# The state part of a fused sandwich block reordered, and its decay rows made by bf16 matmuls of the transposed sums

## The chip, the cores and the metric

One core of one Trainium2 chip runs the whole program. The metric is device time in microseconds (us) from the program's start to its end. Engines: PE (TensorE), DVE (VectorE), ACT (ScalarE), POOL (GpSimd), and SP, which issues the DMAs.

## The reference

The input is 8 sequences of 1024 tokens with 256 features. A state-space mixer with residual and normalisation is followed by a feed-forward part, which adds a dense path and a product-key mixture of 1024 experts. The change touches the mixer's chunked scan alone (chunks of 128 tokens, 8 heads, state of 128 x 64 a head):

```python
a = dtc * A
cum = jnp.cumsum(a, axis=2)                       # running sums inside a chunk
diff = cumT[..., :, None] - cumT[..., None, :]
decay = where(mask, exp(where(mask, diff, 0)), 0)  # [head, token, token]
scores = einsum('bclhg,bcshg->bchls', Cc, Bc) * decay * dtT
Y_intra = einsum('bchls,bcshp->bclhp', scores, Xc)
w = jnp.exp(cum[:, :, -1:, :] - cum) * dtc
S = einsum('bcshg,bcshp->bchgp', Bc * w[..., None], Xc)
dlast = jnp.exp(cum[:, :, -1, :])                  # H <- dlast * H + S, chunk after chunk
Y_inter = einsum('bclhg,bchgp->bclhp', Cc * exp(cum)[..., None], Hprev)
y = Y_intra + Y_inter + D_skip[:, None] * Xc
```

## The kernel before, in words

The 8192 tokens go in 32 groups of 256 tokens, two chunks of 128 each (c = 0 and 1). Each engine runs its own stream, written out by hand in a function `do_group(g, e, f, n)`; semaphores tie the streams together. Three groups are in flight: group g is in the mixer, e = g-1 in the feed-forward's first half, f = g-2 in its second half, and n = g+1 has its input normalised. The loop over g runs from 3 to 30, and the groups at both ends are written out. Nothing plans the order but the order of the calls, and an engine stands still when the head of its stream waits.

In PE's stream a group begins with ten pairs of projection tiles (`mixer_pair`, L1340), between which the feed-forward matmuls of e and f lie. ACT starts the convolution of each pair (`acc`, L694), DVE adds three taps (`mixer_conv`, L998 and L1008), and ACT applies silu (L675). Into this stretch fall on PE the running sums (`mixer_cum`: two small fp32 matmuls with `da`), on ACT their copy `cum` (L703), and on POOL `ncum` (L449), after which POOL waits for DVE's statistics of the next input (L359). Then comes the state part:

- PE `mixer_X(g, c)` (L1391) transposes X into a ring bank, and `mixer_rows(g, c)` (mask L1376, L1379) makes for each head a 128 x 128 block of running sums: an fp32 matmul whose stationary operand is one column of `da`, repeated 128 times, and whose moving operand is the triangle `tri`. ACT `mixer_decay` (L723) makes `Ldec` of it, eight exponentials a chunk.
- PE `mixer_B` transposes B, ACT copies it to `Btok` (L741), PE `mixer_scores` (L1423) makes the scores, and DVE `mixer_scores` (L1024) multiplies them with `Ldec` into `sL`.
- PE `mixer_Yi` (L1413) multiplies with the state H; DVE `mixer_state` (L1034) scales it into `yv`. PE `mixer_Yn` (L1448, the skip term, and L1452) needs `DX` and `Xdt` of POOL and `sL`. DVE `mixer_gate` (L1045, L1048) adds and gates, and ACT squares the gated value (L757).
- PE `mixer_S` (L1432) makes the chunk's state term of `Btok` and `Xw`. POOL `mixer_decay` scales H (L484), DVE `mixer_step` (L1040) adds. H must be up to date before Yi of the next chunk.
- PE `mixer_yT` (L1461) and `mixer_out` (L1471) end the group; the next group's first pair follows.

POOL also makes the expert weights `Em` of e (`weigh`, L535, four heads in a row), once DVE has finished `ffn_choose` (L1125 to L1151), for which ACT makes the exponentials `ee`. `tail_root` on POOL (L508, L510) gives the scale with which DVE ends group f (`ffn_store`, L1191). DVE also masks and multiplies the expert weights (`ffn_mask` L1168, `ffn_times` L1177).

In the texts "Yn(1)" is PE's `mixer_Yn` for c = 1, and so on.

## Time and profile before

| what | value |
|---|---|
| median of 3 runs | 3009.18 us (2999.34, 3009.18, 3031.3) |
| the profiled execution: its own time | 3042.37 us |
| its span | 3040.6 us |
| mean granted PE clock | 0.963 |
| busy PE, DVE, ACT, POOL | 92%, 83%, 57%, 66% |
| chain that ended last, by engine | PE 43%, DVE 23%, ACT 13%, POOL 10%, issue 9% |

A timeline row reads: start in us from the span's start, duration, engine, line of the kernel, operation, what it writes and reads, how many instructions were merged, and in brackets how long the engine had been idle before and what released it. An fp32 matmul shows as two records. The granted clock PEclk is 1.00 at 2.4 GHz and 0.50 at 1.2 GHz.

### The profile page before, as it was taken

Reading aid. Unit: us, or ns where it says so; the run is one execution under the profiler, and the core shown is the slowest. Engines: PE = TensorE matmul, PEld = TensorE weight load, DVE = VectorE, ACT = ScalarE, POOL = GpSimd, SP = SyncE. Lnnn points to the kernel's source line nnn. Section 1 sums busy time; section 2 is a strip of 40 time slices with the busy share of each in tenths; the row PEclk is TensorE's granted clock in tenths of the full one; section 3 lists DMA queues with packets and bytes.
Section 4 is the critical chain, followed back from the end, with each engine's and each line's share of the span. In section 5 each row is a group of like instructions: output and inputs, shape, how many; then the busy total and the mean of one; then the engine's idle time right before and its main releaser. Section 6 shows DMA issues by size and latency. Waiting matters only on the chain.

```text
span 3040.6 us, 50162 instructions
## 1 busy us (share of the span) xinstructions
PE 2806.7 (92%) x14784; PEld 2295.6 (75%) x14784; DVE 2522.2 (83%) x6406; ACT 1722.3 (57%) x3560; POOL 2016.2 (66%) x2388
## 2 busy tenths in 40 slices
PE   5899999999999999999999999999999999999985
PEld 4777777777777777877777777777777777777763
DVE  4588888888888888888888888888888888888874
ACT  4465556655665655556655565555566555556542
POOL 3287667676677676667676667676667676676755
PEclk9999999999999999999999999999999999999997
DMA  3000000000000000000000000000000000000000
GB/s 124 8 8 11 8 7 7 10 10 10 7 7 10 7 10 10 10 3 7 10 10 10 3 10 7 10 10 10 3 10 7 10 10 10 3 10 7 8 4 7
DMA packets 28183, 34.24 MB, mean 11 GB/s; under 512 B 2672, under 2 KB 27248, under 8 KB 27440
## 3 DMA queue, kind: packets, MB, share of 16 engines
q1 hardware_dynamic: 28144, 33.77, 3.4%
q8 instruction: 19, 0.31, 0.0%
q14 instruction: 20, 0.16, 0.0%
HBM read 25.37 MB, written 8.39 MB: 11 GB/s over the span
## 4 chain that ended last, share of the span: by engine, by line
PE 43%; DVE 23%; ACT 13%; POOL 10%; issue 9%; ACTq 1%; DMA 0%; DVEq 0%; SPq 0%; POOLq 0%
DVE acc L1008 9%; PE bank L1340 8%; POOL Em L535 7%; PE bank L1546 7%; PE bank L1471 4%; PE bank L1359 4%; PE products L1504 4%; PE bank L1423 3%; PE bank L1413 3%; ACT Em L824 2%; ACT WT L834 2%; DVE s L1097 2%; PE bank L1452 2%; PE bank L1495 2%; PE bank L1432 2%
## 5 line engine op out<-in xcount | busy, mean ns | idle before, releaser
L1008 DVE SCALAR_TENSOR_TENSOR acc<-bank,cw,acc 128x253 f32<-128x253 f32 (+2 forms) x1920 | 774.3, 473 | 0.0
L1340 PE MATMUL bank<-hT,w_in 128*128 128x256 f32 x2560 | 608.5, 383 | 11.6 <-DVE acc L1008 10.9
L1340 PEld LDWEIGHTS bank<-hT,w_in 128*128 128x128 f32 x2560 | 485.0, 192 | 117.8 <-issue 44.4
L535 POOL TENSOR_TENSOR Em<-ee 128x1024 f32<-128x1024 f32 x256 | 519.4, 2054 | 28.7 <-issue 28.7
L1168 DVE SCALAR_TENSOR_TENSOR Em<-Em,p 128x1024 f32<-128x1024 f32 x256 | 371.5, 1451 | 0.0
L550 POOL TENSOR_TENSOR W<-W,Em 128x1024 f32<-128x1024 f32 x128 | 335.9, 2624 | 8.6 <-ACT Em L824 0.3
L824 ACT ACTIVATE Em<-Em,rden 128x1024 f32<-128x1024 f32 x256 | 292.5, 1143 | 64.6 <-DVE Em L1177 63.0
L694 ACT ACTIVATE acc<-bank,cb,cw 128x256 f32<-128x256 f32 x640 | 325.2, 561 | 0.0
L1177 DVE TENSOR_TENSOR Em<-Em,products 128x1024 f32<-128x1024 f32 x256 | 311.0, 1215 | 4.5
L675 ACT ACTIVATE xbcT<-acc 128x512 f32<-128x512 f32 x320 | 200.6, 627 | 102.5 <-DVE acc L1008 102.2
L1504 PE MATMUL products<-w_de,h2T 128*128 128x512 f32 x512 | 235.4, 603 | 23.0 <-DVE Em L1177 23.0
L1423 PE MATMUL bank<-xbcT 128*128 128x128 f32 x1024 | 161.1, 322 | 100.5 <-ACT Btok L741 100.5
L1519 PE MATMUL bank<-h2T,w_up 128*128 128x256 f32 x1024 | 242.2, 380 | 1.4 <-ACT sim L796 0.7
L1554 PE MATMUL bank<-w_ue,WT 128*128 128x256 f32 x1024 | 233.8, 382 | 2.1 <-ACT WT L834 2.1
L359 POOL TENSOR_SCALAR ve<-mv 128x2 f32<-128x2 f32 x32 | 9.0, 280 | 341.0 <-DVE mv L976 341.0
L1546 PE MATMUL bank<-w_down,hid 128*128 128x256 f32 x1024 | 233.8, 382 | 0.0
L1423 PEld LDWEIGHTS bank<-xbcT 128*128 128x128 f32 x1024 | 146.2, 228 | 115.7 <-ACT Btok L741 115.7
L1519 PEld LDWEIGHTS bank<-h2T,w_up 128*128 128x128 f32 x1024 | 194.7, 190 | 28.6 <-ACT sim L796 1.5
L1546 PEld LDWEIGHTS bank<-w_down,hid 128*128 128x128 f32 x1024 | 194.2, 192 | 28.6 <-issue 0.7
L1554 PEld LDWEIGHTS bank<-w_ue,WT 128*128 128x128 f32 x1024 | 193.8, 192 | 28.1 <-ACT WT L834 2.5
L685 ACT ACTIVATE halo<-bank 128x6 f32<-128x6 f32 x320 | 56.0, 175 | 273.2 <-PE bank L1340 273.1
L484 POOL TENSOR_TENSOR H<-H,ecum 128x512 f32<-128x512 f32 x64 | 66.7, 1042 | 201.6 <-PE bank L1413 201.6
(177 smaller groups left out, 5799.8 us busy)
## 6 DMA issues: line engine op xcount, KB each, us to landing
x_in<-x_dram SPq DMA_DIRECT2D x32, 256.0 KB, 2.7
x_res<-x_dram SPq DMA_DIRECT2D x32, 256.0 KB, 2.6
out_dram<-f SPq DMA_DIRECT2D x32, 256.0 KB, 2.2
w_in<-in_wT_dram SPq DMA_DIRECT2D x1, 3080.0 KB, 13.0
w_up<-upT_dram SPq DMA_DIRECT2D x1, 1024.0 KB, 15.7
w_de<-down_eT_dram SPq DMA_DIRECT2D x1, 1024.0 KB, 17.7
w_down<-downT_dram SPq DMA_DIRECT2D x1, 1024.0 KB, 19.7
w_ue<-up_e_dram SPq DMA_DIRECT2D x1, 1024.0 KB, 21.8
```

The lines of the kernel that those rows point to most:

```text
L535: nc.gpsimd.tensor_tensor(Em[:, k], bc(ee[:, k, 0:XD], 2, KEYS), bc(ee[:, k, XD:XD + KEYS], 1, XD), ALU.mult).then_inc(E_done.sem, 1)
L550: nc.gpsimd.tensor_tensor(W[:], flat[0] if h == 1 else W[:], flat[h], ALU.add)\
L694: last = nc.scalar.activation(acc[:, r, a], ps[:, a * TOK:(a + 1) * TOK], ACT.Identity, scale=cw[:, t, TAPS - 1:TAPS], bias=cb[:, t:t + 1])
L824: nc.scalar.activation(flat, flat, ACT.Silu, scale=rden[:, c, h:h + 1]).then_inc(Zs_done.sem, 1)
L1008: ins = V.scalar_tensor_tensor(acc[:, r, a, ahead:], ps[:, a * TOK:(a + 1) * TOK - ahead], cw[:, t, k:k + 1], acc[:, r, a, ahead:], ALU.mu ...
L1168: V.scalar_tensor_tensor(flat, flat, p8[:, k, TOP - 1:TOP], flat, ALU.is_ge, ALU.mult)\
L1340: last = mm(ring[j % 2][:, a * TOK:(a + 1) * TOK], w_in[:, k, at:at + P], hT[:, k, :], start=k == 0, stop=k == DK - 1)
L1423: last = mm(pairb[q][:, i * P:(i + 1) * P], xbcT[:, INNER // P + h, c * P:(c + 1) * P], xbcT[:, INNER // P + HEADS + h, c * P:(c + 1) * P] ...
L1504: last = mm(fA[:, q * 512:(q + 1) * 512], h2T[:, k, c * P:(c + 1) * P], w_de[:, k, q * 512:(q + 1) * 512], start=k == 0, stop=k == DK - 1)
L1519: last = mm(yb[:, a * TOK:(a + 1) * TOK], w_up[:, k, (2 * j + a) * P:(2 * j + a + 1) * P], h2T[:, k, :], start=k == 0, stop=k == DK - 1)
L1546: last = mm(f0[:, c * D:(c + 1) * D], hid[:, i, c * P:(c + 1) * P], w_down[:, i, :], start=False, stop=False)
L1554: last = mm(f0[:, c * D:(c + 1) * D], WT[:, 4 * q + i, :], w_ue[:, 4 * q + i, :], start=False, stop=c == CH - 1 and q == 1 and i == 3)
```

## The change

1. **Rows by bf16.** `da` is widened to 128 columns: four blocks of 32, each with the 16 columns (chunk, head) and 16 zeros. PE's `mixer_cum` gets a third fp32 matmul, `da` transposed times `tri`, which gives the running sums transposed, four times over. ACT copies them to `cumT`. A new `mixer_parts` on POOL turns them into `cum_parts` in bf16 by six 128 x 128 instructions, each waiting for the one ahead: copy to bf16, remainder of two blocks, remainder again, so that the blocks hold three parts whose sum is exact. The row matmul is then a bf16 one: `pick`, a constant 0/1 column repeated 128 times, times `cum_parts`. PE's `mixer_rows(g, 0)` waits for `parts_done`.
2. **Order of the state part.** PE: `B(0)` and `Yi(0)` go ahead of `hT(n)`, and `S(0)` goes from behind `rows(1)` to ahead of `Yn(0)`. ACT: `B(0)` goes ahead of `ffn_out` and `hT(n)`, and `B(1)` ahead of `square(0)`. DVE: `conv(8)` goes ahead of `ffn_best(e, 1)`, `state(0)` ahead of `scores(0)`, and `step(0)` ahead of `ffn_store(f)` and `gate(0)`. POOL: the scaling of H for c = 0 goes from behind the four heads of `weigh(e, 0)` to behind the first.
3. **Start.** POOL writes the constants `pick`, `minus_a`, `minus_b` and clears `da` once.

The diff, cut (the declarations and constants of item 3 are left out):

```diff
@@ POOL, mixer_dt @@
-                nc.gpsimd.tensor_tensor(da[:], dts[:], bc(neg_a[:], 1, CH), ALU.mult).then_inc(da_done.sem, 1)
+                nc.gpsimd.tensor_tensor(dta[:], dts[:], bc(neg_a[:], 1, CH), ALU.mult).then_inc(own_pool, own.one())
+                pool.wait_ge(own_pool, own.n)
+                nc.gpsimd.tensor_copy(da[:, :, 0:CH * HEADS], bc(dta[:].rearrange("p c h -> p (c h)"), 1, 4))\
+                    .then_inc(da_done.sem, 1)
@@ POOL @@
+            def mixer_parts(g):
+
+                if later(g):
+                    pool.wait_ge(rows_ps.sem, rows_ps.at(g - 1, 2 * CH - 1))
+                pool.sem_inc(arrived_pool, 1)
+                nc.gpsimd.tensor_copy(cum_parts[:], cumT[:]).then_inc(own_pool, own.one())
+                pool.wait_ge(own_pool, own.n)
+                nc.gpsimd.tensor_scalar(cum_rest[:], cum_parts[:], minus_a[:, 0:1], None, ALU.mult)\
+                    .then_inc(own_pool, own.one())
+                pool.wait_ge(own_pool, own.n)
+                nc.gpsimd.tensor_tensor(cum_rest[:], cum_rest[:], cumT[:], ALU.add).then_inc(own_pool, own.one())
+                pool.wait_ge(own_pool, own.n)
+                nc.gpsimd.tensor_copy(cum_parts[:], cum_rest[:]).then_inc(own_pool, own.one())
+                pool.wait_ge(own_pool, own.n)
+                nc.gpsimd.tensor_scalar(cumT[:], cum_parts[:], minus_b[:, 0:1], None, ALU.mult)\
+                    .then_inc(own_pool, own.one())
+                pool.wait_ge(own_pool, own.n)
+                nc.gpsimd.tensor_tensor(cum_parts[:], cum_rest[:], cumT[:], ALU.add).then_inc(parts_done.sem, 1)
@@ POOL, do_group @@
                 if a:
                     mixer_cum(g)
+                    mixer_parts(g)
...
                 if b:
-                    weigh(e, 0, 0, 1, 2, 3)
+                    weigh(e, 0, 0)
                 if a:
                     mixer_decay(g, 0)
+                if b:
+                    weigh(e, 0, 1, 2, 3)
@@ ACT, mixer_cum @@
                 if later(g):
                     act.wait_ge(ecum_done.sem, ecum_done.at(g - 1))
+                    act.wait_ge(parts_done.sem, parts_done.at(g - 1))
                 nc.scalar.activation(cum[:, 0:3:2],
-                                     yb[:, 0:2 * CH * HEADS].rearrange("p (a c h) -> p a c h", a=2, c=CH), ACT.Copy)\
-                    .then_inc(cum_sb.sem, 1)
+                                     yb[:, 0:2 * CH * HEADS].rearrange("p (a c h) -> p a c h", a=2, c=CH), ACT.Copy)
+                nc.scalar.activation(cumT[:], yb[:, P:2 * P], ACT.Copy).then_inc(cum_sb.sem, 1)
@@ ACT, do_group @@
                     mixer_norm(n, e)
+                if a:
+                    mixer_B(g, 0)
+                if c:
+                    ffn_out(f)
+                if n is not None:
                     mixer_hT(n)
-                if c:
-                    ffn_out(f)
-                if a:
-                    mixer_B(g, 0)
                 if a:
                     mixer_move(g, 1)
                     mixer_decay(g, 1)
+                    mixer_B(g, 1)
                     mixer_square(g, 0)
-                    mixer_B(g, 1)
@@ DVE, do_group @@
-                conv(7)
+                conv(7, 8)
                 if b:
                     ffn_best(e, 1)
-                conv(8, 9)
+                conv(9)
...
                 if a:
+                    mixer_state(g, 0)
                     mixer_scores(g, 0)
-                    mixer_state(g, 0)
                 if b:
                     ffn_last(e, 0)
                     ffn_mask(e, 0, 0)
+                if a:
+                    mixer_step(g, 0)
                 if c:
                     ffn_store(f)
                 if a:
                     mixer_gate(g, 0)
-                    mixer_step(g, 0)
@@ PE, mixer_cum @@
-                mm(yb[:, 0:n], tri[:], da[:].rearrange("p c h -> p (c h)"), start=True, stop=True)
-                mm(yb[:, n:2 * n], ones[:], da[:].rearrange("p c h -> p (c h)"), start=True, stop=True)\
+                mm(yb[:, 0:n], tri[:], da[:, 0, 0:n], start=True, stop=True)
+                mm(yb[:, n:2 * n], ones[:], da[:, 0, 0:n], start=True, stop=True)
+                mm(yb[:, P:2 * P], da[:].rearrange("p a b -> p (a b)"), tri[:], start=True, stop=True)\
                     .then_inc(cum_ps.sem, 1)
@@ PE, mixer_rows @@
+                if c == 0:
+                    pe.wait_ge(parts_done.sem, parts_done.at(g))
                 for q in range(2):
...
-                        last = mm(pairb[q][:, i * P:(i + 1) * P], da[:, c, h:h + 1].to_broadcast([P, P]), tri[:],
+                        k = c * HEADS + h
+                        last = mm(pairb[q][:, i * P:(i + 1) * P], pick[:, k:k + 1].to_broadcast([P, P]), cum_parts[:],
                                   start=False, stop=i == 3)
@@ PE, do_group @@
+                if a:
+                    mixer_B(g, 0)
+                    mixer_Yi(g, 0)
                 if n is not None:
                     mixer_hT(n, e)
                 if a:
-                    mixer_B(g, 0)
                     mixer_scores(g, 0)
-                    mixer_Yi(g, 0)
+                    mixer_S(g, 0)
                     mixer_Yn(g, 0, e, n)
                     mixer_X(g, 1)
                     mixer_rows(g, 1, f)
-                    mixer_S(g, 0)
                     mixer_B(g, 1)
                     mixer_scores(g, 1)
                     mixer_Yi(g, 1)
```

## Rows read from the trace of the kernel before

**Rows 1.** The top of the page: busy time by engine
```profile
PE 2806.7 (92%) x14784; PEld 2295.6 (75%) x14784; DVE 2522.2 (83%) x6406; ACT 1722.3 (57%) x3560; POOL 2016.2 (66%) x2388
```

**Rows 2.** Busy time by stretch: two single groups, then 29 together (engines, PEclk, DMA)
```profile
core 0: us, PE busy (x) PEld busy (x) DVE busy (x) ACT busy (x) POOL busy (x), PEclk, DMA share, GB/s
833.57:922.66 89.09, 84.31 (x462) 68.98 (x461) 77.93 (x201) 53.52 (x111) 63.36 (x74) 1.00 0.03 9
1471.43:1564.98 93.55, 88.78 (x462) 72.90 (x461) 78.92 (x201) 53.52 (x111) 62.85 (x74) 0.95 0.03 8
195.72:2853.83 2658.11, 2520.43 (x13371) 2067.11 (x13369) 2276.47 (x5804) 1552.01 (x3219) 1829.01 (x2146) 0.97 0.03 9
```

**Rows 3.** Timeline of PE, the group from 833.57 (start, us, line, work)
```profile
872.72 0.66 PE L1391 MATMUL bank<-ident,xbcT 128*128 128x128 f32 x4 [0.62 <-DVE acc L1008]
...
877.52 0.38 PE L1376 MATMUL bank<-mask_b,ident_b 128*128 128x512 bf16 x1
877.74 1.05 PE L1379 MATMUL bank<-tri,da 128*128 128x128 f32 x8
...
879.74 3.62 PE L1554 MATMUL bank<-w_ue,WT 128*128 128x256 f32 x16
...
899.75 2.05 PE L1423 MATMUL bank<-xbcT 128*128 128x128 f32 x16 [2.60 <-ACT Btok L741]
...
904.29 1.89 PE L1452 MATMUL bank<-Xdt,sL 128*128 128x64 f32 x16
...
911.35 1.97 PE L1471 MATMUL bank<-w_out,yT 128*128 128x256 f32 x8 [0.78 <-ACT yT L765]
913.16 3.62 PE L1340 MATMUL bank<-hT,w_in 128*128 128x256 f32 x16
```

**Rows 4.** Timeline of DVE, the same group
```profile
864.65 2.42 DVE L1008 SCALAR_TENSOR_TENSOR acc<-bank,cw,acc 128x253 f32<-128x253 f32 x6
...
869.98 0.35 DVE L998 SCALAR_TENSOR_TENSOR acc<-bank,cw,halo_sum 128x3 f32<-128x3 f32 x2
...
879.57 0.62 DVE L1125 TENSOR_TENSOR prod<-ee 128x64 f32<-128x64 f32 x4 [2.92 <-ACT ee L809]
...
894.83 1.45 DVE L1191 TENSOR_SCALAR f<-f,mvf,rsf 128x256 f32<-128x256 f32 x2 [0.92 <-POOL rsf L510]
...
898.38 0.68 DVE L1040 TENSOR_TENSOR H<-H,bank 128x512 f32<-128x512 f32 x1
...
901.31 1.28 DVE L1024 TENSOR_TENSOR sL<-bank,Ldec 128x512 f32<-128x512 f32 x2
```

**Rows 5.** Timeline of ACT, the same group
```profile
867.03 1.01 ACT L694 ACTIVATE acc<-bank,cb,cw 128x256 f32<-128x256 f32 x2
...
875.29 0.63 ACT L675 ACTIVATE xbcT<-acc 128x512 f32<-128x512 f32 x1 [1.96 <-DVE acc L1008]
...
876.31 1.07 ACT L834 ACTIVATE WT<-bank 128x512 f32<-128x512 f32 x2
...
893.48 2.25 ACT L723 ACTIVATE Ldec<-bank,ncum 128x128 f32<-128x128 f32 x8 [0.51 <-PE bank L1379]
898.49 0.63 ACT L757 ACTIVATE zs<-yv 128x512 f32<-128x512 f32 x1 [2.77 <-DVE yv L1048]
```

**Rows 6.** Timeline of POOL, the same group
```profile
876.39 0.29 POOL L359 TENSOR_SCALAR ve<-mv 128x2 f32<-128x2 f32 x1 [10.32 <-DVE mv L976]
...
884.35 7.48 POOL L535 TENSOR_TENSOR Em<-ee 128x1024 f32<-128x1024 f32 x4 [0.63 <-issue]
...
894.08 0.71 POOL L510 TENSOR_TENSOR rsf<-vf,half_neg 128x2 f32<-128x2 f32 x1
...
896.45 1.46 POOL L473 TENSOR_TENSOR Xw<-Xdt,ecum 128x512 f32<-128x512 f32 x1 [0.64 <-PE bank L1432]
```

**Rows 7.** Timeline of PE, the group from 1471.43
```profile
1537.60 3.78 PE L1423 MATMUL bank<-xbcT 128*128 128x128 f32 x16 [2.58 <-ACT Btok L741]
1541.18 3.51 PE L1413 MATMUL bank<-H,xbcT 128*128 128x64 f32 x16
```

**Rows 8.** Groups of instructions: the one bf16 copy of this size on POOL
```profile
L349 POOL CAST ident_b<-ident 128x128 bf16<-128x128 f32 x1 | 0.3, 290 | 0.1
```

More of the change, by code:

```diff
@@ L150, in sandwich @@
         dts = sb("dts", [P, CH, HEADS])
-        da = sb("da", [P, CH, HEADS])
+        da = sb("da", [P, 4, 2 * CH * HEADS])
+        cumT = sb("cumT", [P, P])
+        cum_rest = sb("cum_rest", [P, P])
+        cum_parts = sb("cum_parts", [P, P], BF16)
+        minus_a = sb("minus_a", [P, 1])
+        minus_b = sb("minus_b", [P, 1])
+        pick = sb("pick", [P, CH * HEADS], BF16)
         cum = sb("cum", [P, 3, CH, HEADS])
@@ L235, in sandwich @@
         dt_ps, dt_sb, dt_abs, dte_done, da_done = (sig(n) for n in ("dt_ps", "dt_sb", "dt_abs", "dte_done", "da_done"))
+        parts_done = sig("parts_done")
         cum_ps, cum_sb, cum_diff, ecum_done = (sig(n) for n in ("cum_ps", "cum_sb", "cum_diff", "ecum_done"))
@@ L332, in _ @@
             nc.gpsimd.memset(H[:], 0.0).then_inc(own_pool, own.one())
+            nc.gpsimd.memset(da[:], 0.0).then_inc(own_pool, own.one())
+            nc.gpsimd.memset(pick[:], 0.0).then_inc(own_pool, own.one())
+            nc.gpsimd.memset(minus_a[:], -1.0).then_inc(own_pool, own.one())
+            nc.gpsimd.memset(minus_b[:], -1.0).then_inc(own_pool, own.one())
             nc.gpsimd.memset(minus1[:], -1.0).then_inc(own_pool, own.one())
@@ L347, in _ @@
                 .then_inc(own_pool, own.one())
+            for first, minus in ((64, minus_a), (96, minus_b)):
+                nc.gpsimd.affine_select(out=minus[:], in_=minus[:], compare_op=ALU.is_ge, fill=0.0,
+                                       base=-first, pattern=[[0, 1]], channel_multiplier=1)\
+                    .then_inc(own_pool, own.one())
+            for block in range(3):
+                pool.wait_ge(own_pool, own.n)
+                nc.gpsimd.affine_select(out=pick[:], in_=pick[:], compare_op=ALU.not_equal, fill=1.0,
+                                       base=-32 * (block + 1), pattern=[[-1, CH * HEADS]], channel_multiplier=1)\
+                    .then_inc(own_pool, own.one())
             pool.wait_ge(own_pool, own.n)
@@ L449, in mixer_cum @@
                 nc.gpsimd.tensor_scalar(ncum[:], cum[:, 0], -1.0, None, ALU.mult).then_inc(cum_diff.sem, 1)
+            def mixer_parts(g):
[5 more added lines that the diff above has]
+                nc.gpsimd.tensor_scalar(cum_rest[:], cum_parts[:], minus_a[:, 0:1], None, ALU.mult)\
+                    .then_inc(own_pool, own.one())
+                pool.wait_ge(own_pool, own.n)
[4 more added lines that the diff above has]
+                nc.gpsimd.tensor_scalar(cumT[:], cum_parts[:], minus_b[:, 0:1], None, ALU.mult)\
+                    .then_inc(own_pool, own.one())
+                pool.wait_ge(own_pool, own.n)
+                nc.gpsimd.tensor_tensor(cum_parts[:], cum_rest[:], cumT[:], ALU.add).then_inc(parts_done.sem, 1)
             def mixer_keep(g):
@@ L913, in do_group @@
                     mixer_norm(n, e)
-                    mixer_hT(n)
+                if a:
+                    mixer_B(g, 0)
                 if c:
                     ffn_out(f)
-                if a:
-                    mixer_B(g, 0)
+                if n is not None:
+                    mixer_hT(n)
                 if a:
```

## The prediction

> **What bounds the kernel now.** I read the page first: PE is busy 92% of the span, DVE 83% [rows 1], so PE looks like the bound. Then I cut the span into groups at the first down-projection matmul of each. 29 groups take 2658.11 us, 91.66 each; one takes 89.09 at a granted clock of 1.00, another 93.55 at 0.95 with the same instructions [rows 2]. PE is busy 84.31 of the 89.09, so it stands for 4.78 a group even where the clock is full. The timeline of PE shows where: 0.62 before X(0), 0.79 before scores(0), 2.60 before scores(1), 0.78 before out(1) [rows 3]. The wait of 2.60 is the one that matters twice. In the group of 93.55 the clock fell to its 1.2 GHz level while PE stood there: scores(1) takes 3.78 instead of 2.05, and Yi(1) 3.51 [rows 7]. The clock thus costs 0 to 4.46 us a group, 2.57 in the mean (91.66 - 89.09).
>
> What ends the 2.60? Follow it back in the fast group. Scores(1) needs Btok, ACT copies that behind the square at 898.49, the square needs DVE's gate, the gate lies behind the store of f at 894.83, that waits for POOL's root (894.08 + 0.71), POOL makes it behind four expert weights and the scaling of H (884.35 on), those wait for DVE's choice, the choice for ACT's exponentials (879.57, idle 2.92), and ACT for the last convolution at 875.2 [rows 4 to 6]. So one chain over DVE, ACT, POOL and DVE again runs from conv(9) to the gate. DVE goes on from it, without a wait, to scores(1), 901.31 to 902.59 [rows 4]. PE's Yn(1) begins at 904.29 [rows 3]. PE and that chain are 1.70 us apart there: this is the number on which the forecast rests.
>
> **The change part by part.**
>
> *Order on ACT and PE.* B(1) ahead of the square cuts the link from the gate to scores(1). S(0) ahead of Yn(0) only moves 1.7 us of PE's work. PE's way to Yn(1): it comes to rows(0) at 877.52, less 0.40 (0.62 of waiting gone, 0.22 more for the new matmul of the transposed sums: two records at the pace of the row matmuls, whose eight take 0.89) = 877.12 [rows 3]. Rows(0) needs ACT's copies of WT, of which the first now ends some 0.54 into 876.31 + 1.28 = 878.13 (the 1.28 is below) [rows 5], so it starts at 878.2. From rows(0) to Yn(1) were 904.29 - 877.52 = 26.77, of it 3.39 waiting, so 23.38 of work; less 1.8 for the rows (next item). New waits: B(1) needs the exponentials of rows(1), which take 2.25 on ACT and were hidden behind S(0) [rows 5]; at that pace its two halves wait about 0.8 and 0.6, and the scores 0.15. Sum: 878.2 + 23.4 - 1.8 + 1.6 = 901.4 at Yn(1). PE would be 2.9 us early.
>
> *Rows by bf16.* Two blocks of mask and four row matmuls take 879.74 - 877.52 = 2.22, the mask 0.22 of each [rows 3], so four fp32 row matmuls take 0.89. The mask is itself bf16, 512 columns in 0.22, so 128 columns in bf16 can take 0.055, and no more than the fp32 0.22. Between 0 and 0.67 saved a block; I take 0.45, near the mask row but with room for a weight load each, four blocks: 1.8 a group. The Trainium skill (TensorE: Matmul & The Clock Gate, Back-to-back issue gap) gives about 81 ns for a pair of weight load and matmul of 128 columns; by it four take 0.32 and a group saves 2.3. No trace here shows it, and neither end of this moves the sum, since PE waits at Yn(1) anyway.
>
> *Parts on POOL.* Six instructions of 128 x 128, each behind a wait: between the copy's 0.29 [rows 8] and a 128 x 512's 1.46 [rows 6] each, so 1.7 to 8.8; I take 2.5. They lie in POOL's idle time of 10.32 before 876.39 [rows 6], and rows(0) comes 11 us after the sums. Even the upper end is covered, and POOL can gain nothing there either, since its next work waits for DVE. The new wait of PE ahead of rows(0) would hold all of PE's stream if it came late; it is met some 8 us early. ACT's extra copy of the sums costs about one of the eight exponentials (2.25 / 8 = 0.28 [rows 5]); PE's up(2) waits for it but stands behind pair 8, which takes longer, and ACT's next work of its own is ready 1 us later only by pair 8. From zero to 0.28, zero taken. The widened `da` adds one small copy (0.3) ahead of a chain with several us to spare. DVE's convolutions beside it read the same memory: 2.42 for conv(7) with POOL idle [rows 4]; I take no slowing. The Trainium skill (GPSIMD Engine Reference, Specifications) speaks against it: POOL's memory interface is shared with DVE, with contention where DVE reads two inputs from it. The convolution reads one of its two from a bank, and if it did slow, DVE's chain would lengthen by as much.
>
> *Order on DVE.* Here the change costs. Conv(8) now follows conv(7), which ends at 864.65 + 2.42 = 867.07 or just under, since it overlaps. But ACT begins pair 8 only at 867.03 and ends at 868.04 [rows 5], plus the 0.22 of the new matmul: conv(8) starts at about 868.3. Before, the second ffn_best filled that time and conv(8) began at 869.98 [rows 4]. So DVE stands 1.3 us, ffn_best moves behind, and conv(9) ends 1.28 later. It earns the 0.62 before X(0). Everything on the chain follows 1.28 later: WT, exponentials, choice, four weights and the scaling (the same five instructions in another order, so the same sum), root, store. DVE's step(0) leaves the chain for idle time ahead of the store: -0.60. So DVE's scores(1) end at 902.59 + 1.28 - 0.60 = 903.27. POOL's Xw(1) loses its 0.64 of waiting for S(0) [rows 6] but starts 1.28 later; its skip term is ready at about 900.1, no bound.
>
> *Sum.* Yn(1) starts at 903.35, not 904.29: 0.94 earlier, and behind it PE's own order to the next group's first pair is unchanged (904.29 to 913.16 [rows 3]). A group at full clock takes 89.09 - 0.94 = 88.15. PE's stall of 2.60 is not gone: it has moved from scores(1) to Yn(1), some 3 us in two pieces around the skip matmul.
>
> *The clock.* With a longer stall, and 1.6 us of waiting a few us ahead of it, I expect that the clock falls in every group and not in most, and what stands behind the stall is all PE's own path. I take the row of the costliest group, 4.46, against 2.57 in the mean before. A group: -0.94 + 1.89 = +0.95; 30 groups: +28.5 us. The profiled execution took 3042.37, so 3071, a factor of 1.0094; on the median of 3009.18 (1.1% below the profiled one) 3037 us. Start and end are as before: POOL's added constants lie under the loading of the weights.
>
> **The rivals.**
>
> *The clock costs what it did.* The stall has the same length within half a us, so 2.57 again: -0.94 x 30 = -28 us, 3014 profiled, 2981 in the median. For it: the falls before depended on where in time the stall came. Against: more waiting in all.
>
> *The clock does not fall,* because the waits are now in pieces. Then 88.15 a group, -3.51 x 30 = -105: 2905. For it: two groups at full clock with 2.60 of waiting [rows 3].
>
> *Slower: the clock stays low for all work behind the stall.* Yn(1), yT(0), S(1) and out(0) were 911.35 - 0.78 - 904.29 = 6.28 us [rows 3]; at half rate they cost 6.28 more. 6.28 - 2.57 - 0.94 = +2.77, 30 times +83: 3125 profiled, 3092 in the median. It decides from where the clock costs over 3.51 a group (2.57 + 0.94); over 1% slower from 4.5. For it: before, the work behind the stall was scores(1), here it is mostly 64-column matmuls, and all of it lies on the path. The Trainium skill (TensorE: Matmul & The Clock Gate, HAM oscillation) says that waits inside a loop can throw PE back to the low rate in each turn; the rows of the group of 93.55 agree.
>
> *The chain over DVE and POOL gives way,* and PE alone sets the group: 84.31 - 1.8 + 0.22 of work and 1.6 of waiting, 84.3; -7.3 x 30 = -220: about 2791. Against: none of the chain's waits is removed, only its last link to scores(1).
>
> **How the numbers follow.** Chances: forecast 0.40 (own range 3000 to 3065), clock as before 0.22, clock never low 0.08, slower 0.25, chain gives way 0.05. The range from 2962 to 3092 leaves out the two fast cases and some of the slow one. This kernel's runs differ by 1%, so I call a change under 1% none (2979 to 3039). Faster: half of the second case, the third and the fifth, 0.24. Slower: half of the forecast's range and nearly all of the slow case, 0.42. Same: 0.34.
>
> **What would show it.** On PE: no wait before X(0), about 1 us before rows(0), two short ones before B(1), a wait of over 2 us before Yn(1) and none before scores(1). On DVE: over 1 us of waiting before conv(8), released by ACT, and 2 to 3 us before the store, released by POOL's root. On POOL: the six instructions within its idle time. Windows of a group: 88.2 where the clock is 1.00. I am wrong if Yn(1) does not wait (then the chain was not as tight), if DVE does not stand before conv(8), or if the clock in the groups is above 0.97.

## The result, and the profile after

The changed kernel takes 3157.73 us (median of four runs, 3157.01 to 3158.79), the kernel before 3019.44 us on the same chip (median of four). The ratio is 1.045, with an interval of 1.0395 to 1.0505: slower by 4.5%. The forecast was 3037, with a range from 2962 to 3092. The kernel before varies by about 1% from run to run, and the ratios in this text leave out its slowest runs. The profiled execution took 3157.83, its span is 3156.1 us, its mean clock 0.926 (before: 3042.37, 3040.6, 0.963). The top of the page of after:

```profile
PE 2818.2 (89%) x14336; PEld 2277.6 (72%) x14336; DVE 2593.3 (82%) x6406; ACT 1718.5 (54%) x3592; POOL 2080.8 (66%) x2621
```

Against [rows 1], PE has 448 instructions fewer (14336 instead of 14784) and is still busy for 12 us more. Less work that takes longer is the sign of a slower clock. The windows of after, cut at the same matmul as [rows 2], first one group, then 29 together, then four short stretches inside the one group (columns as in [rows 2]):

```profile
1247.77:1343.34 95.57, 87.40 (x448) 70.78 (x447) 80.86 (x201) 53.41 (x112) 64.92 (x81) 0.93 0.03 8
194.21:2968.10 2773.89, 2536.90 (x12965) 2054.19 (x12963) 2344.77 (x5802) 1549.08 (x3248) 1883.79 (x2349) 0.93 0.03 8
...
1307.50:1316.40 8.90, 6.25 (x46) 4.81 (x43) 6.52 (x8) 3.78 (x13) 8.33 (x8) 1.00 0.08 29
1316.40:1319.90 3.50, 0.02 (x1) 0.05 (x1) 3.50 (x5) 3.25 (x6) 3.50 (x2) 0.53 0.00 0
1319.90:1330.80 10.90, 10.90 (x46) 10.26 (x47) 8.23 (x9) 2.47 (x4) 3.60 (x4) 0.52 0.00 0
1330.80:1343.30 12.50, 11.72 (x53) 8.73 (x51) 8.52 (x20) 5.57 (x11) 5.42 (x7) 1.00 0.00 0
```

The 29 groups take 95.65 us each in the mean, against 91.66. The first five take 95.7 to 96.4, and the rest are alike within 0.1. Inside the group the clock column is 1.00, then 0.53 and 0.52, then 1.00 again: it falls to its 1.2 GHz level while PE stands (0.02 us busy in 3.50) and comes back 14.4 us later. PE in that group, the rows that answer to [rows 3]:

```profile
1292.55 0.39 PE L1427 MATMUL bank<-mask_b,ident_b 128*128 128x512 bf16 x1 [1.26 <-ACT WT L880]
1292.78 0.39 PE L1431 MATMUL bank<-cum_parts,pick 128*128 128x128 bf16 x4
1293.04 0.39 PE L1427 MATMUL bank<-mask_b,ident_b 128*128 128x512 bf16 x1
...
1308.54 0.66 PE L1452 MATMUL bank<-ident,xbcT 128*128 128x128 f32 x4 [0.84 <-ACT Ldec L769]
1309.57 0.66 PE L1452 MATMUL bank<-ident,xbcT 128*128 128x128 f32 x4 [0.38 <-ACT Ldec L769]
1310.06 2.04 PE L1475 MATMUL bank<-xbcT 128*128 128x128 f32 x16
...
1314.89 1.12 PE L1500 MATMUL bank<-DX,ident 128*128 128x512 f32 x2 [1.05 <-DVE yv L1092]
1319.88 3.65 PE L1504 MATMUL bank<-Xdt,sL 128*128 128x64 f32 x16 [3.86 <-DVE sL L1071]
...
1324.17 3.52 PE L1484 MATMUL bank<-Xw,Btok 128*128 128x64 f32 x16
1327.47 3.34 PE L1523 MATMUL bank<-w_out,yT 128*128 128x256 f32 x8
...
1332.03 1.97 PE L1523 MATMUL bank<-w_out,yT 128*128 128x256 f32 x8 [0.78 <-ACT yT L811]
```

Read it from the top. The mask row and the four row matmuls of a block now start 0.23 and 0.26 apart, so four in bf16 take nearly as long as the one mask matmul (both take 0.22 in most blocks of this trace). The waits stand where the prediction put them: 1.26 before rows(0), 0.84 and 0.38 before B(1), none before scores(1), and then two around the skip matmul, 1.05 and 3.86. What follows at 1319.88 runs at half rate: Yn(1) takes 3.65 instead of 1.89, S(1) 3.52, out(0) 3.34. DVE in the same group, as [rows 4]:

```profile
1282.58 0.35 DVE L1045 SCALAR_TENSOR_TENSOR acc<-bank,cw,halo_sum 128x3 f32<-128x3 f32 x2 [1.27 <-ACT acc L739]
...
1304.72 2.92 DVE L1215 SCALAR_TENSOR_TENSOR Em<-Em,p 128x1024 f32<-128x1024 f32 x1
...
1310.55 2.25 DVE L1238 TENSOR_SCALAR f<-f,mvf,rsf 128x256 f32<-128x256 f32 x2 [2.31 <-POOL rsf L552]
1312.83 1.41 DVE L1242 TENSOR_TENSOR f<-f,x_late 128x512 f32<-128x512 f32 x1
...
1316.74 1.79 DVE L1215 SCALAR_TENSOR_TENSOR Em<-Em,p 128x1024 f32<-128x1024 f32 x1
1318.45 1.27 DVE L1071 TENSOR_TENSOR sL<-bank,Ldec 128x512 f32<-128x512 f32 x2
```

Conv(8) waits 1.27 for ACT, as worked out. But the store, which waits 2.31 for POOL's root, then takes 2.25 + 1.41, where [rows 4] has 1.45 for its first part (and 0.69 for its second). The mask ahead of it takes 2.92 (2.06 before), the one behind it 1.79 (1.27 before). POOL, as [rows 6]:

```profile
1280.72 0.29 POOL L479 CAST cum_parts<-cumT 128x128 bf16<-128x128 f32 x1
...
1283.40 0.46 POOL L491 TENSOR_TENSOR cum_parts<-cum_rest,cumT 128x128 bf16<-128x128 f32 x1
1292.00 0.28 POOL L379 TENSOR_SCALAR ve<-mv 128x2 f32<-128x2 f32 x1 [8.15 <-DVE mv L1023]
...
1310.48 1.04 POOL L509 TENSOR_TENSOR Xdt<-Xt,dts 128x512 f32<-128x512 f32 x1
1311.61 1.04 POOL L515 TENSOR_TENSOR Xw<-Xdt,ecum 128x512 f32<-128x512 f32 x1
1312.61 1.09 POOL L535 TENSOR_TENSOR DX<-Xt,head_c 128x512 f32<-128x512 f32 x1
```

The six instructions of the parts lie between 1280.72 and 1283.86, with 8.15 us of idle time left behind them. Look at the last three rows: Xdt, Xw and the skip term run from 1310.48 to 1313.70 without a gap, beside nearly all of DVE's store (1310.55 to 1314.24). In [rows 6] Xw(1) still stood 0.64 for S(0) there. The same place in the trace of before, in which the store's second part begins within that gap:

```profile
894.77 1.04 POOL L467 TENSOR_TENSOR Xdt<-Xt,dts 128x512 f32<-128x512 f32 x1
896.32 0.69 DVE L1195 TENSOR_TENSOR f<-f,x_late 128x512 f32<-128x512 f32 x1
```

Compare who starts first. Xdt starts ahead of the store's first part (894.77 and 894.83) and keeps its 1.04, and that part takes 1.45. The second part starts ahead of Xw (896.32 and 896.45) and keeps its 0.69, and Xw takes 1.46 instead of 1.04. In after, POOL is ahead all the way: its three take 1.04, 1.04 and 1.09, and both parts of the store are long. In these rows, then, it is the later of the two that pays.

**What the 3.9 us of a group are.** From the start of Yn(1) to the first moment at which out(1) could run were 911.35 - 0.78 - 904.29 = 6.28 us in [rows 3]; now they are 1332.03 - 0.78 - 1319.88 = 11.37. The instructions are the same, so the clock costs 5.09 a group. Without it the group of 95.57 would take 90.48, which is 1.39 more than the 89.09 of [rows 2], where the forecast had 0.94 less. So 3.91 = 1.39 (the chain is longer) + 2.52 (the clock, 5.09 against a mean of 2.57).

### The profile page after: what moved, and what is told of

It reads as the page before. It is cut to its first block, busy times and chain, and to the rows that moved or that the text cites. A ratio compares the mean times of both kernels' runs of the same rounds, so it can differ in the third digit from the quotient of the medians.

```text
span 3156.1 us, 49541 instructions
## 1 busy us (share of the span) xinstructions
PE 2818.2 (89%) x14336; PEld 2277.6 (72%) x14336; DVE 2593.3 (82%) x6406; ACT 1718.5 (54%) x3592; POOL 2080.8 (66%) x2621
## 4 chain that ended last, share of the span: by engine, by line
PE 58%; DVE 19%; POOL 10%; issue 8%; ACT 4%; DMA 0%; DVEq 0%; SPq 0%; ACTq 0%; POOLq 0%
PE bank L1388 15%; POOL Em L577 7%; PE bank L1598 7%; PE bank L1523 5%; DVE acc L1055 5%; PE bank L1504 4%; PE bank L1606 4%; PE bank L1571 4%; PE bank L1408 4%; PE products L1556 4%; PE bank L1547 3%; PE bank L1484 3%; DVE Em L1215 2%; DVE Em L1224 1%; PE bank L1513 1%
## 5 line engine op out<-in xcount | busy, mean ns | idle before, releaser
L577 POOL TENSOR_TENSOR Em<-ee 128x1024 f32<-128x1024 f32 x256 | 557.1, 2196 | 28.6 <-PE bank L1465 18.4
L1215 DVE SCALAR_TENSOR_TENSOR Em<-Em,p 128x1024 f32<-128x1024 f32 x256 | 421.8, 1648 | 0.0
L1504 PEld LDWEIGHTS bank<-Xdt,sL 128*128 128x128 f32 x1024 | 170.7, 257 | 156.3 <-issue 156.3
L1504 PE MATMUL bank<-Xdt,sL 128*128 128x64 f32 x1024 | 173.8, 342 | 116.1 <-DVE sL L1071 116.1
L1045 DVE SCALAR_TENSOR_TENSOR acc<-bank,cw,halo_sum 128x3 f32<-128x3 f32 x640 | 109.5, 212 | 123.4 <-ACT acc L739 123.1
L1523 PE MATMUL bank<-w_out,yT 128*128 128x256 f32 x512 | 168.9, 489 | 24.9 <-ACT yT L811 24.9
```

The costliest lines, as they stand in the source:

```text
L577: nc.gpsimd.tensor_tensor(Em[:, k], bc(ee[:, k, 0:XD], 2, KEYS), bc(ee[:, k, XD:XD + KEYS], 1, XD), ALU.mult).then_inc(E_done.sem, 1)
L1215: V.scalar_tensor_tensor(flat, flat, p8[:, k, TOP - 1:TOP], flat, ALU.is_ge, ALU.mult)\
L1504: last = mm(yb[:, h * HD:(h + 1) * HD], sL[:, h, :], Xdt[:, h * HD:(h + 1) * HD], start=False, stop=h == HEADS - 1)
L1523: last = mm(pairb[0][:, c * D:(c + 1) * D], yT[:, i * P:(i + 1) * P], w_out[:, i, :], start=i == 0, stop=i == INNER // P - 1)
```

## The experiments

There are two questions: which part of the change costs what, and why the chain over DVE and POOL came 2.3 us later than forecast. A third came up on the way: what is the clock worth by itself? The kernels with idle matmuls answer that one: PE multiplies `ident` by a slice of weights into a free bank while it would stand anyway. "Before" in each comparison is the kernel before on the same chip.

**e1_rows_only**: the kernel before, with the bf16 rows and POOL's parts, and its own order on all engines. All of the row part of the diff and none of the moves.

```diff
-last = mm(pairb[q][...], da[:, c, h:h + 1].to_broadcast([P, P]), tri[:], start=False, stop=i == 3)
+last = mm(pairb[q][...], pick[:, k:k + 1].to_broadcast([P, P]), cum_parts[:], start=False, stop=i == 3)
```

> The order of before with the rows made by bf16 matmuls of the transposed sums (the new POOL work, ACT copy and PE wait included). Order theory (the loss comes from the new order: the chain over DVE and POOL ends later at Yn(1), PE waits there 4.9 us a group and its clock is low behind that wait in every group): the chain of before is unchanged, the 1.8 us that PE saves turn into a longer wait before scores(1), so full-clock groups stay at about 89 us and only the clock may fall more often, up to 4.5 us a group: 3020 to 3080 us. Rows theory (the six POOL instructions and the wait for them cost the time): about 3140 us or more, with PE waiting before rows(0) for POOL or POOL late in its chain.

Measured: 3068.94 (3062.37 to 3073.81), ratio 1.011 [1.008, 1.0141]. PE's wait before scores(1), in one group of e1:

```profile
1098.70 3.40 PE L1472 MATMUL bank<-xbcT 128*128 128x128 f32 x16 [5.71 <-ACT Btok L785]
1101.94 1.90 PE L1462 MATMUL bank<-H,xbcT 128*128 128x64 f32 x16
```

It was 2.60 in [rows 3] and is 5.71. That is 3.11 more, and what the bf16 rows save on PE is in it: none of it shortens the group. But why is the kernel slower by 1.1%? S(0), DVE and POOL in the same group:

```profile
1090.16 1.95 PE L1481 MATMUL bank<-Xw,Btok 128*128 128x64 f32 x16
...
1092.32 1.04 POOL L509 TENSOR_TENSOR Xdt<-Xt,dts 128x512 f32<-128x512 f32 x1
1092.39 2.25 DVE L1236 TENSOR_SCALAR f<-f,mvf,rsf 128x256 f32<-128x256 f32 x2 [2.04 <-POOL rsf L552]
```

S(0) stands where it stood in the order of before, but PE comes to it earlier by what the rows save. It ends before Xdt begins, so the gap on POOL is closed here too, and the store takes 2.25 + 1.41, with POOL's Xw from 1093.44 on beside it. That is 1.52 more on the chain in each group. The clock now falls in every group, but in most only over scores(1) (3.40 instead of 2.05, about 1.4; Yi(1) behind it takes its full-rate 1.90), which is less than the mean of 2.57 in before. A group takes 92.69 in the mean, 1.03 more than in before: the slowed store accounts for it, and the clock doesn't. The expected range was met, but the expectation that the chain stays as it was, and that only the clock costs, was not.

**e2_order_only**: the changed kernel with fp32 rows and without the parts; the row part of the diff is taken back, all moves stay.

```diff
-last = mm(pairb[q][...], pick[:, k:k + 1].to_broadcast([P, P]), cum_parts[:], start=False, stop=i == 3)
+last = mm(pairb[q][...], da[:, c, h:h + 1].to_broadcast([P, P]), tri[:], start=False, stop=i == 3)
```

> The new order with the fp32 row matmuls of before. Order theory: nearly the time of the changed kernel, 3110 to 3165 us; PE comes to Yn(1) some 1.3 us later (the fp32 rows take 2 x 0.67 us more there), so the wait before Yn(1) is 3 to 4 us instead of 4.9, and the clock still falls in each group. Rows theory: back at the time of before, about 3020 us.

Measured: 3114.73 (3112.54 to 3119.88), ratio 1.027 [1.0242, 1.0298]. The wait has moved to Yn(1) and is 2.7 long, in every group:

```profile
1113.42 1.97 PE L1456 MATMUL bank<-Xdt,sL 128*128 128x64 f32 x16 [2.73 <-DVE sL L1027]
```

DVE's store takes 2.25 + 1.41 in that group, as in e1: the moves without the rows close the gap on POOL as well. The order alone costs 2.7%, and the rows on top of it another 1.4% (3157.73 / 3114.73). Most of the loss is the order's.

**e3_conv8_back**: the changed kernel with conv(8) behind the second ffn_best again, as before.

```diff
-                conv(7, 8)
+                conv(7)
                 if b:
                     ffn_best(e, 1)
-                conv(9)
+                conv(8, 9)
```

> The changed kernel with conv(8) behind the second ffn_best again, as before. If DVE's wait of 1.3 us before conv(8) is on the path, conv(9) and all behind it come 1.3 us earlier, the wait at Yn(1) shrinks from 4.9 to about 3.6 us and a group loses 1.3 us: 30 groups, 39 us, 3119 us, the clock still low behind the wait. If PE alone sets the group (X(0) then waits 0.6 us), 3158 us or a little more.

Measured: 3150.9 (3147.45 to 3155.28), ratio 1.0385 [1.0357, 1.0414]. It gives only 7 of the 38 us that 1.28 a group would give, so neither of the two expected times (3119 and 3158) came. PE in one group:

```profile
1120.92 3.64 PE L1504 MATMUL bank<-Xdt,sL 128*128 128x64 f32 x16 [4.26 <-DVE sL L1071]
...
1128.52 3.73 PE L1523 MATMUL bank<-w_out,yT 128*128 128x256 f32 x8
```

From the end of conv(9) to the end of scores(1) are 29.40 us here and 28.94 in after, so some 0.8 of the 1.28 reach Yn(1). But now the low stretch covers all of out(0) (3.73, in after 3.34) and the second transpose (0.99, in after 0.60): 0.78 is lost to the slow clock, and nothing is left in this group. How long a group is at the low clock isn't fixed by its stall alone.

**e4_fill_wait**: the changed kernel with four idle matmuls in the wait before Yn(1). Their result is never read.

```diff
+                if c:
+                    pe.wait_ge(X_sb.sem, X_sb.at(g, 1))
+                    for _ in range(4):
+                        mm(ring[1][:], ident[:], w_in[:, 0, 0:INNER], start=True, stop=True)
                 pe.wait_ge(Xdt_done.sem, Xdt_done.at(g, c))
```

> The changed kernel with four idle fp32 matmuls of 512 columns (3.5 us of PE work, result never read) put between the skip matmul and the head matmuls of Yn(1), in the time in which PE waits. Everything else is the same work in the same order. Clock theory (5.1 of the 95.6 us of a group are the half-rate clock behind the wait): the clock stays at 1.00, a group takes about 90.5 us, 3005 us. If the low clock were hidden by DVE's work: no gain, 3158 us, or up to 3170 where the added work is late.

Measured: 3017.2 (3016.01 to 3018.16, five runs), ratio 0.9946 [0.9925, 0.9967]. One group:

```profile
1018.80:1109.38 90.58, 85.82 (x456) 67.67 (x455) 80.00 (x203) 53.53 (x113) 66.24 (x81) 1.00 0.03 9
```

The chain is untouched, and the clock is 1.00 all through. The group takes 90.58, where 90.48 was worked out above. One group in six takes 91.6, with the clock at 0.98. So the clock's cost is shown by taking it away: 140 us of the whole kernel. That is as much as the whole loss, but it isn't the cause of all of it, for the kernel before loses some to the clock as well (e8).

**e6_pool_after_store**: the changed kernel in which POOL's Xdt(1), Xw(1) and skip term wait until DVE's store is done. It takes away the work beside the store, and delays POOL by the length of the store.

```diff
                 if a:
+                    if c:
+                        pool.wait_ge(o_done.sem, o_done.at(f))
                     mixer_scale(g, 1)
```

> The changed kernel, with POOL's second scaling (Xdt, Xw, DX for c = 1) held back until DVE has stored f. If DVE's store (2.25 + 1.41 us, against 1.45 + 0.69 before the change) is slowed by POOL's three instructions beside it, it is back at about 1.45 + 0.69 us, and DVE's scores(1) end up to 1.4 us earlier after POOL's root than in the changed kernel. If the store is slow for another reason, it stays at 3.6 us. The time itself: 3115 to 3160 us, since the wait at Yn(1) is still over 3 us and the clock falls in it.

Measured: 3119.51 (two runs, 3118.6 and 3120.41), ratio 1.0292 [1.0198, 1.0386]. DVE's store in one group:

```profile
1105.54 0.73 DVE L1240 TENSOR_SCALAR f<-f,mvf,rsf 128x256 f32<-128x256 f32 x2 [2.30 <-POOL rsf L552]
1106.31 0.69 DVE L1244 TENSOR_TENSOR f<-f,x_late 128x512 f32<-128x512 f32 x1
```

The store takes 0.73 + 0.69 instead of 2.25 + 1.41, with the same instructions on the same data. Over all groups the mean of one half of the store falls from 1166 to 459 ns, the second part from 1368 to 692 ns. That POOL's work beside it is what slows DVE is thereby shown. The kernel gains only about 1.2% by it, since PE now waits for POOL:

```profile
1110.96 1.10 PE L1502 MATMUL bank<-DX,ident 128*128 128x512 f32 x2 [2.12 <-POOL DX L535]
1113.24 3.61 PE L1506 MATMUL bank<-Xdt,sL 128*128 128x64 f32 x16 [1.18 <-DVE sL L1073]
```

The skip matmul comes 2.12 later and the heads 1.18 more: 3.30 in place of 4.91, and the clock still falls.

**e7_store_late**: the changed kernel, with DVE's gate(0), first product and scores(1) ahead of the store, so that they don't queue behind its wait for POOL's root.

```diff
-                if c:
-                    ffn_store(f)
                 if a:
                     mixer_gate(g, 0)
                 if b:
                     ffn_times(e, 0, 0)
-                    ffn_mask(e, 0, 1)
                 if a:
                     mixer_scores(g, 1)
+                if c:
+                    ffn_store(f)
+                if b:
+                    ffn_mask(e, 0, 1)
```

> The changed kernel with one more reordering on DVE: gate(0), times(0,0) and scores(1) go ahead of ffn_store(f), which alone waits for POOL's root; mask(0,1) goes behind the store. Chain theory (Yn(1) waits for DVE's scores(1) because these stand behind the store and POOL's root): scores(1) end some 7 us earlier, Yn(1) does not wait, the clock stays up in most groups, and a group takes about 87 us: 2892 us, up to 2960 where the clock still falls in part of them. If instead the rows part or PE's own work were the bound: over 3100 us.

Measured: 3019.41 (ten runs, 3017.53 to 3024.28), ratio 1.0013 [0.9986, 1.004]. PE:

```profile
1076.44 1.89 PE L1505 MATMUL bank<-Xdt,sL 128*128 128x64 f32 x16
...
1082.87 3.75 PE L1524 MATMUL bank<-w_out,yT 128*128 128x256 f32 x8 [2.35 <-ACT yT L811]
```

Yn(1) doesn't wait any more. But the next link gives way: out(0) waits 2.35 for ACT's yT(0), and in three of four groups the clock falls there. ACT in the same group:

```profile
1081.09 1.15 ACT L870 ACTIVATE Em<-Em,rden 128x1024 f32<-128x1024 f32 x1 [0.69 <-DVE Em L1224]
1082.15 0.58 ACT L811 ACTIVATE yT<-bank 128x512 f32<-128x512 f32 x1
```

It makes yT(0) behind an expert product that waits for DVE, and DVE now makes that product behind the store. The expected 2892 to 2960 left this queue out. A stall taken from one place of PE's stream was paid at the next.

**e8_before_fill**: the kernel before, with three idle matmuls in its 2.60 us of waiting.

```diff
                     mixer_B(g, 1)
+                    pe.wait_ge(X_sb.sem, X_sb.at(g, 1))
+                    for _ in range(3):
+                        mm(ring[1][:], ident[:], w_in[:, 0, 0:INNER], start=True, stop=True)
                     mixer_scores(g, 1)
```

> The kernel before, with three idle fp32 matmuls of 512 columns (2.65 us of PE work, result never read) between B(1) and scores(1), where PE waits 2.6 us. Clock theory: the clock no longer falls, all groups take 89.1 to 89.3 us instead of 91.7 in the mean, 2.5 x 30 = 75 us less: about 2950 us. If the clock's fall were not due to that wait: no gain, 3030 us or slightly more.

Measured: 2965.21 (2964.39 to 2966.41), ratio 0.9784 [0.9715, 0.9853]. Every group is now as the fast one of [rows 2]:

```profile
1000.90:1090.01 89.11, 86.75 (x465) 69.95 (x468) 77.94 (x203) 53.52 (x112) 63.37 (x74) 1.00 0.03 9
```

Both kernels with their waits filled, e4 and e8, stand as 0.9946 to 0.9784, a ratio of 1.017. Of the 4.5%, then, about 1.7% is the longer chain and the rest the clock.

**e9_store_late_conv8**: e7 with e3's edit, conv(8) back behind the second ffn_best.

```diff
-                conv(7, 8)
+                conv(7)
...
-                conv(9)
+                conv(8, 9)
```

> As the kernel with the late store, and conv(8) behind the second ffn_best again. Without a wait for POOL's root DVE works nearly without a pause from the choice to gate(1), so the 1.3 us that conv(8) loses early should show in the group: 0.6 to 1.3 us less than with the late store alone, 20 to 40 us. If PE's wait of 0.6 us before X(0) is what counts: 0 to 20 us more.

Measured: 2927.17 (2922.35 to 2930.87), ratio 0.9652 [0.9583, 0.9721]. PE:

```profile
1150.36 1.97 PE L1524 MATMUL bank<-w_out,yT 128*128 128x256 f32 x8 [1.10 <-ACT yT L811]
1153.32 0.66 PE L1514 MATMUL bank<-ident,yv 128*128 128x128 f32 x4 [1.00 <-DVE yv L1095]
```

The same edit that gave 7 us in e3 gives 92 here (20 to 40 were expected), 3.1 a group where the chain can give 1.28 at most. It shortens out(0)'s wait from 2.35 to 1.10, and with that the clock stays up: the mean clock goes from 0.957 to 0.982.

**e10_yT_early** and **e11_same_fp32_rows**: e9 with ACT's yT(0) ahead of the expert product, and the same order with fp32 rows and no parts.

```diff
                 if b:
                     tail_keep(e)
-                    ffn_experts(e, 0, 0, 1)
                 if a:
                     mixer_yT(g, 0)
+                if b:
+                    ffn_experts(e, 0, 0, 1)
+                if a:
                     mixer_square(g, 1)
```

> The kernel with the late store and conv(8) back, and on ACT yT(0) ahead of the two expert activations it stood behind. In that kernel PE waits 1.1 us (2.4 us in the kernel with the late store alone) before out(0) for ACT's yT(0), and 1.0 us before yT(1) for DVE. Theory: out(0) goes without a wait, but yT(1) then waits for DVE's gate(1) for the whole 2.1 us, since the gate is DVE's; so the gain is only what the clock gives, 0 to 0.7 us a group: 2905 to 2930 us. Rival: if the wait before out(0) is itself on the path, 1.1 us a group: about 2895 us.

> The same order as the kernel with yT(0) early, but with the fp32 row matmuls of before, without the six POOL instructions, the third matmul of the sums and its copy. Order theory: the rows part is worth what PE saves where PE is the bound, 2 x 0.67 us behind X(0) less 0.22 us: if PE does not wait behind them, this kernel takes 0.5 to 1.5 us a group more than the other, 15 to 45 us. Rows theory (the POOL work costs more than PE saves): it is faster than the other.

Measured: e10 2948.09 (2946.33 to 2949.17), ratio 0.975 [0.9719, 0.978]; e11 2952.03 (2948.88 to 2952.81), ratio 0.9761 [0.973, 0.9792]. E10 is slower than e9, which was not expected. PE before its second transpose, and two windows next to each other:

```profile
1153.01 0.66 PE L1516 MATMUL bank<-ident,yv 128*128 128x128 f32 x4 [2.29 <-DVE yv L1097]
1154.44 3.75 PE L1526 MATMUL bank<-w_out,yT 128*128 128x256 f32 x8 [0.78 <-ACT yT L811]
```

```profile
1078.40:1168.93 90.53, 85.04 (x445) 68.14 (x447) 80.82 (x208) 53.58 (x113) 67.03 (x84) 0.96 0.04 11
1168.93:1255.90 86.97, 81.81 (x445) 66.17 (x447) 79.38 (x195) 53.40 (x113) 64.63 (x79) 1.00 0.02 7
```

Its waits of 1.1 and 1.0 have become a single one of 2.29, and behind that the clock falls in every second group. E11 has 2.6 us more of row matmuls in the same order. Its wait there is 1.82, and it stays at full clock:

```profile
1082.25:1171.03 88.78, 84.48 (x459) 68.83 (x462) 80.71 (x201) 53.55 (x112) 62.48 (x74) 1.00 0.03 9
```

E9's groups at full clock take 87.56, and e10's own 86.97, so at full clock the bf16 rows are worth some 88.78 - 87.56 = 1.2 to 88.78 - 86.97 = 1.8 us a group. Neither pair is clean: e9 has yT(0) in another place, and e10's group follows one in which the clock fell. E10's two groups take (90.53 + 86.97) / 2 = 88.75: the one that falls gives it all back, and e10 and e11 are the same within 0.2%, where 15 to 45 us were expected between them.

**e12_e9_fill**: e9 with one idle matmul before out(0) and one before the second transpose, into a bank that nothing reads before it is written again.

```diff
             def mixer_yT(g, c):
+                if c:
+                    mm(pairb[1][:], ident[:], w_in[:, 0, 0:INNER], start=True, stop=True)
...
+                if c == 0:
+                    mm(pairb[1][:], ident[:], w_in[:, 0, 0:INNER], start=True, stop=True)
                 pe.wait_ge(yT_sb.sem, yT_sb.at(g, c))
```

> The kernel with the late store and conv(8) back, with one idle fp32 matmul of 512 columns (0.88 us, result never read) in each of PE's waits before out(0) (1.1 us) and before yT(1) (1.0 us). Clock theory: the groups of 88.7 us fall to the 87.57 us that most have already, 10 to 20 us less in all: 2905 to 2920 us, granted clock over 0.985. If the falls there come from the waits before B(1), which are not filled: no change, 2927 us.

Measured: 2917.13 (2914.95 to 2918.43), ratio 0.9636 [0.9597, 0.9675], the fastest of all, and 10 us below e9, which ran on another chip; the ratios alone (0.9636 and 0.9652) don't tell them apart. The groups do: all take 87.5, where e9 had 12 of 29 at 88.6 to 89.3, and the mean clock is 0.990.

**e13_before_store_late**: the kernel before, with only e7's move on DVE. No other engine's order changes, and the rows stay fp32.

```diff
-                if c:
-                    ffn_store(f)
                 if a:
                     mixer_step(g, 0)
...
                     ffn_times(e, 0, 0)
-                    ffn_mask(e, 0, 1)
                 if a:
                     mixer_scores(g, 1)
+                if c:
+                    ffn_store(f)
+                if b:
+                    ffn_mask(e, 0, 1)
```

> The kernel before with one thing changed: on DVE gate(0), step(0), times(0,0) and scores(1) go ahead of ffn_store(f). Chain theory (the link from POOL's root over the store to the gate made PE's wait of 2.6 us): the gate ends 3 us earlier, scores(1) goes without a wait, the clock stays up in most groups, and a group takes 86.5 to 88.5 us against 91.7: 2870 to 2930 us, without any part of the change. If the wait before scores(1) had another cause: 3020 us.

Measured: 2971.37 (2970.27 to 2974.34), ratio 0.9818 [0.9778, 0.9858], clock 0.988. PE:

```profile
1063.28 2.05 PE L1424 MATMUL bank<-xbcT 128*128 128x128 f32 x16 [0.25 <-ACT Btok L741]
...
1072.54 1.97 PE L1472 MATMUL bank<-w_out,yT 128*128 128x256 f32 x8 [0.65 <-ACT yT L765]
1075.50 0.66 PE L1462 MATMUL bank<-ident,yv 128*128 128x128 f32 x4 [1.00 <-DVE yv L1048]
```

Scores(1) waits 0.25 instead of 2.60, but 0.65 and 1.00 come up before out(0) and the second transpose. At full clock a group takes 89.2, no less than the 89.09 of before: the 2.6 us were not won as time, they were spread into pieces, and 1.8% was won because the clock holds through the pieces in four of five groups. The expected 2870 to 2930 took them for time won.

## Why the prediction was wrong, by its own steps

**What held.** The outline of the mechanism did. The 2.60 was not removed, it went to Yn(1) (e2 shows it with the order alone). Conv(8)'s wait is 1.27 (1.28 worked out), the wait before rows(0) 1.26 (about 1.1), those before B(1) 0.84 and 0.38 (0.8 and 0.6). From conv(8) to the store are 1310.55 - 1282.58 = 27.97 us; the forecast's own terms give 894.83 + 1.28 - 868.3 = 27.81. POOL's parts take 3.14 (2.5 taken) in idle time, of which 8.15 was left. The clock falls in every group, as forecast.

**The step that failed: the chain from the store to scores(1).** The prediction took DVE's instructions there at their old lengths, less 0.60 for step(0): 902.59 - 894.83 - 0.60 = 7.16 us. It measured 1318.45 + 1.27 - 1310.55 = 9.17. The difference of 2.01 is that of the store's two parts (2.25 - 1.45 and 1.41 - 0.69, together 1.52) and of the mask (1.79 - 1.27 = 0.52). The reason was in the sentence before the sum: "POOL's Xw(1) loses its 0.64 of waiting for S(0) [rows 6] ... no bound". It isn't a bound for anyone who waits for Xw, but it put Xw and the skip term on POOL ahead of the store's second part, and e6 shows that POOL's work beside it is what the store pays for. More than one item of the change closes this gap. The moves do it without the rows (e2 has the long store): S(0) ahead of Yn(0) was costed at nothing because it "only moves 1.7 us of PE's work", and conv(8)'s wait brings POOL's Xdt and Xw later past S(0). No run separates these two. The rows do it without the moves (e1): the time that they save on PE brings S(0) forward. The mask's 0.52 fits the same reading: in e1, where POOL stands during it, it takes 1.28. But no run takes it apart. The Trainium skill (GPSIMD Engine Reference, Specifications) says that POOL's memory interface is shared with DVE, with contention for a DVE instruction that reads two inputs from it or runs in a mode with two ports. The prediction weighed it for the parts beside the convolutions, where nothing slowed (2.42 for conv(8), in after as before), and not for the store, where it decided. What remains of the 2.33 (1.39 + 0.94) is 0.32: 0.16 in the chain ahead of the store, 0.08 in conv(8)'s start (1282.58 - 1247.77 = 34.81 us into the group, 868.3 - 833.57 = 34.73 in the forecast), and 0.08 between scores(1) and Yn(1).

**A slip in the forecast: the length of the wait.** The two pieces of waiting were put at some 3 us and measured 4.91. By the forecast's own times they were 903.35 - 901.4 = 1.95; 2.9 was PE's lead over the old start of Yn(1). The later chain adds 2.2 to the 1.95, and the rows, which save 0.8 more on PE than taken, add the rest. The price of the clock was argued from "a longer stall", and by these terms it was a shorter one than the 2.60. At 1.95 nothing on record says that the clock falls: in e11 it doesn't, behind a wait of 1.82. So that it fell in every group was in part luck. That the first piece ends with DVE's gate(0), which stands behind the store, is a second wait on the same chain and costs nothing extra.

**A term too small: the clock.** 4.46 was taken, from the costliest group of before; it measured 5.09 and, in e4, its removal was worth (3157.73 - 3017.2) / 30 = 4.7. Of +3.91 a group against a forecast of +0.95, 2.33 is the chain and 0.63 the clock. The rival "the clock stays low for all work behind the stall" named this mechanism and had 6.28 as its end. Its price of 3092 fell short, though 6.28 was more than the clock cost, because it kept the forecast's 0.94 of gain.

**The rows.** They save 2.6 on PE, not 1.8: two blocks take 0.93 instead of 2.22, so 0.65 a block. "Neither end of this moves the sum, since PE waits at Yn(1) anyway" was half right. PE's saved time didn't shorten the group, but it lengthened the wait and brought S(0) forward, and e1 shows 1.1% lost by that. The Trainium skill (TensorE: Matmul & The Clock Gate, Back-to-back issue gap) has about 81 ns for a weight load and matmul of this size; by the trace it is 0.22 / 4 = 0.055 us here, and the measurement decides.

**Left open.** What decides whether the clock falls behind a given wait. Waits of 2.73 (e2) bring it down in every group, of 2.60 (before) in 25 of 29, of 2.35 (e7) in three of four, of 2.29 (e10) in every second, of 1.82 (e11) in none, but of 1.1 and 1.0 close together (e9) in 12 of 29; nothing finer was tried. Nor was the mask beside POOL's weights (2.92) taken apart by a run of its own. That the engine that starts first keeps its length is read from rows and was not tried by itself.

## What to carry to other kernels

Before you count a move as free, ask what the closed gap had kept apart: list which instructions of DVE and POOL now run side by side, note which starts first, and price the other at the slowed length. Ask it of saved work too, since what comes earlier on one engine can close a gap on another (e1). When PE waits for a chain over other engines, less work on PE only lengthens the wait, and behind a wait of over 2 us the slow clock can cost more than the wait itself; so shorten the chain first, above all by putting what waits for another engine (here the store, behind POOL's root) behind what PE is waiting for. Then look at the next wait in PE's stream, since two short ones were cheaper than one long one, and where one can't be removed, idle matmuls in it are worth trying: by themselves they made the old kernel about 2% faster (e8).

## What the runs showed of the hardware

- POOL beside DVE slowed DVE's store by much: an instruction over 128x256 takes 459 ns on average in e6 and 1166 beside POOL in after, one over 128x512 692 and 1368.
- In the rows shown the instruction that started first kept its length: the store's second part, ahead of Xw by 0.13 us in before, took 0.69, and Xw took 1.46 instead of 1.04.
- Four bf16 matmuls of 128 columns with their weight loads took 0.22 us in most blocks of after, as long as one of 512 columns; four in fp32 took 0.89.
- Behind a stall that is repeated, the groups came out at one length (95.55 to 95.6 in most of after), or at two in turn (e10: 90.53 and 86.97).
- With 2.6 us less of row matmuls on PE a group (e10 against e11) the kernel took the same time within 0.2%, and the clock fell in every second group.
